# Moving the rotary addition of the local attention from GpSimd to VectorE, and moving three pieces of work to later steps of the stage loop

## The reference

```
def _L0_ffn_ref(x, wqkv, q_scale, k_scale, wo, ln_g, ln_b, w1, b1, w2, b2):
    def l2norm(t):
        return t / jnp.clip(jnp.linalg.norm(t, axis=-1, keepdims=True), 1e-12)
    ...
        q = q * cos * scale + rotate_half(q) * sin * scale
        k = k * cos / scale + rotate_half(k) * sin / scale
    ...
    def _layer(x, ...):
        h = shift_token(x)
        q, k, v = jnp.split(h @ wqkv, 3, axis=-1)
        q = l2norm(q) * qs
        k = l2norm(k) * ksc
        q, k = rotary_xpos(q, k)
        x = x + local_attention(q, k, v) @ wo
        ...
        return x + (a * gelu(g)) @ w2 + b2

x = L0_attn_x
xn = _layernorm(x)
x = x + _L0_attn_ref(xn, ...) * _silu(_L0_ffn_ref(xn, ...))
xn = _layernorm(x)
x = x + _L1_attn_ref(xn, ...) * _silu(_L1_ffn_ref(xn, ...))
```

## Time and profile before

| | |
|---|---|
| three runs | 3027.77, 3028.91, 3041.24 us (median 3028.91) |
| the profiled execution | 3018.12 us, its span 3016.2 us, mean granted TensorE clock 0.959 |
| stage -1 | 0 to 87 us |
| retention stages 0 to 7 | 87 to some 1170 us, 136 us each |
| latent stages 8 to 14 | some 1170 to 2237 us, 157 or 160 us each from stage 9 on |
| stage 15, then the experts | 2237 to 2390 us, then to the end |

### The profile page before, as it was taken

One profiled execution on the slowest core, in us unless ns is written; L12 is line 12 of the kernel. 1 busy time (PEld: TensorE's weight loads), 2 busy tenths in 40 slices (PEclk: granted clock), 3 DMA queues, 4 the chain that ended last, 5 costly groups with the idle time before them and its releaser, 6 DMA issues.

```text
span 3016.2 us, 42014 instructions
## 1 busy us (share of the span) xinstructions
PE 2759.6 (91%) x15582; PEld 1865.9 (62%) x15582; DVE 1613.1 (53%) x3810; ACT 1216.7 (40%) x2249; POOL 1046.1 (35%) x735
## 2 busy tenths in 40 slices
PE   6999999999999999899999999999987899999992
PEld 3575656566565656545555555556554488989992
DVE  6656566675656557666667667675754520000004
ACT  4444444535344445444444445454543242212221
POOL 5423243443423244353534445352532221111113
PEclk9999999999999999999999999999998799999996
DMA  3000000000001011001010101010001367989886
GB/s 135 11 22 18 25 22 32 15 25 15 25 22 47 26 42 65 15 4 50 4 50 4 50 4 43 11 43 12 29 18 36 142 253 269 348 327 350 331 325 209
DMA packets 85908, 261.84 MB, mean 87 GB/s; under 512 B 10668, under 2 KB 49916, under 8 KB 67020
## 3 DMA queue, kind: packets, MB, share of 16 engines
q1 hardware_dynamic: 79228, 241.38, 22.0%
q0 software_dynamic: 6480, 17.77, 1.6%
HBM read 210.81 MB, written 44.11 MB: 85 GB/s over the span
## 4 chain that ended last, share of the span: by engine, by line
PE 74%; DVE 13%; DMA 5%; issue 3%; SPq 2%; POOL 2%; ACT 1%; POOLq 0%; DVEq 0%; ACTq 0%
PE s_pD L705 21%; PE s_pA L705 17%; PE s_pD L1153 7%; PE s_pA L1138 6%; PE s_pD L859 4%; PE s_pD L777 3%; PE s_pA L755 3%; PE s_pA L764 3%; DMA s_w_w<-rows_s 3%; DVE s_pairs L1722 2%; DVE s_qk L1624 2%; PE s_pA L869 2%; PE s_pA L716 2%; PE s_pA L744 1%; DMA s_z<-s_cur 1%
## 5 line engine op out<-in xcount | busy, mean ns | idle before, releaser
L1455 POOL TENSOR_TENSOR s_qk<-s_qk,s_rrec 128x1024 f32<-128x1024 f32 (+1 forms) x128 | 223.5, 1746 | 594.2 <-DVE s_rrec L1630 594.1
L705 PE MATMUL s_pA<-s_w_wqkv,s_curT 128*128 128x512 f32 x768 | 370.5, 625 | 5.6 <-ACT s_curT L1183 3.7
L1207 ACT ACTIVATE s_qk<-s_qk,s_mx 128x256 f32<-128x256 f32 (+1 forms) x512 | 239.8, 471 | 61.6 <-DVE s_mx L1624 60.9
L705 PEld LDWEIGHTS s_pA<-s_w_wqkv,s_curT 128*128 128x128 f32 x768 | 148.5, 199 | 187.4 <-issue 174.6
L1722 DVE TENSOR_SCALAR s_pairs<-s_pD 128x1024 f32<-128x1024 f32 (+1 forms) x192 | 193.6, 1039 | 130.2 <-PE s_pD L859 128.2
L2071 DVE COPY s_w_wo<-s_pD 128x256 f32<-128x256 f32 x71 | 30.0, 423 | 413.8 <-PE s_pD L1124 413.8
L859 PE MATMUL s_pD<-s_mixer 32*128 32x512 f32 (+3 forms) x1024 | 188.8, 486 | 49.8 <-DVE s_pairs L1722 34.3
L1545 POOL DMA_INDIRECT acc_s<-s_w_w,s_sq x71 | 68.5, 964 | 472.0 <-ACT s_w_w L1396 464.7
L1449 POOL TENSOR_TENSOR s_rinv<-s_ssq,s_half 128x16 f32<-128x16 f32 x64 | 204.7, 3198 | 6.4
L859 PEld LDWEIGHTS s_pD<-s_mixer 32*128 32x128 f32 x1024 | 97.1, 196 | 153.4 <-issue 55.1
L1445 POOL TENSOR_TENSOR s_qk<-s_qk,s_rot 128x1024 f32<-128x1024 f32 x64 | 150.7, 2355 | 112.4 <-DVE s_qk L1607 112.4
(11 more groups left out here) (270 smaller groups left out, 5833.3 us busy)
## 6 DMA issues: line engine op xcount, KB each, us to landing
s_qkT<-in_m_w SPq DMA_DIRECT2D x48, 1024.0 KB, 5.1
s_v_tm<-in_m_w SPq DMA_DIRECT2D x24, 1024.0 KB
s_rot<-in_m_w SPq DMA_DIRECT2D x24, 1024.0 KB, 5.6
s_w_wqkv<-in_m_w SPq DMA_DIRECT2D x23, 1024.0 KB
s_qk<-in_m_w SPq DMA_DIRECT2D x23, 1024.0 KB, 5.5
s_w_w<-rows_s SPq DMA_DIRECT2D x71, 129.0 KB
s_cur<-in_x SPq DMA_DIRECT2D x8, 512.0 KB, 3.3
xn_s<-s_cur SPq DMA_DIRECT2D x8, 512.0 KB, 2.6
```

What stands on the lines that cost most here:

```text
L705: last = nc.tensor.matmul(out, lhs(c), rhs(c), start=(c == 0), stop=(c == n - 1))
L1207: last = nc.scalar.activation(pi, pi, ACT.Exp, scale=-1.0, bias=mx[:, u, i:i + 1], accum_out=rsum[:, u, i:i + 1])
L1455: nc.gpsimd.tensor_tensor(pi, pi, rrec[:, u, :].unsqueeze(2).broadcast_to((P, 4, 256 - lo)), ALU.mult).then_inc(p_rdy, 1)
```

## The change

The rotary addition moves to VectorE, and `tiny` goes: its bound becomes an upper bound of 1e12 on the reciprocal norm, inside the scaling. In the stage loop, `down_projection`'s second half moves from u = 1 to 2 in stages 8 to 14 and what hangs on it moves by a step; the transposes of the tokens and the projections behind them move from u = 4 to 5; `input_stats` and `input_apply` move from u = 6 and 8 to u = 8 and 10. The diff, cut (the ring lists and ScalarE's loop follow the same moves):

```
-            def down_projection(b):
+            def down_projection(b, i):
...
-                        down_projection(k)
+                        down_projection(k, 0)
+                        if s.ret or s.last:
+                            down_projection(k, 1)
+                    if s.lat and not s.last and u == 2:
+                        down_projection(k, 1)
...
-                    if s.lat and u == 4:
+                    if s.lat and u == 5:
                         for i in range(2):
                             pe.wait_ge(norm_x, NT * b + 2 * i + 2)
                             pair_transposes("x1T", b, i, lambda t, c: xn[:, t, c * P:(c + 1) * P])
...
                 if w == 1:
-                    act.wait_ge(rinv_rdy, NT * b + 3)
+                    act.wait_ge(rot_rdy, NT * b + NT)
...
-            def rotary_sum(b, t):
-                pool.wait_ge(rot_rdy, NT * b + t + 1)
-                nc.gpsimd.tensor_tensor(qk[:, t, :], qk[:, t, :], rot[:, t % 2, :], ALU.add)
...
-                    if s.ret and k + 2 < B and u == 6:
-                        reciprocal_roots(var_1, rstd_1, k + 2)
-                    if s.lat and u == 2:
-                        reciprocal_roots(var_x, rstd_x, b)
...
                     if s.ahead and u < 2 * NT:
                         scale_probabilities(k + 1, u)
+                    if s.lat and u == 2:
+                        reciprocal_roots(var_x, rstd_x, b)
+                    if s.ret and k + 2 < B and u == 8:
+                        reciprocal_roots(var_1, rstd_1, k + 2)
...
-                if t >= 2:
-                    dve.wait_ge(rinv_rdy, NT * b + t - 1)
...
-                nc.vector.tensor_tensor(o1, o1, Ct[:, t].unsqueeze(2).broadcast_to((P, 2, 8, DH)), ALU.mult).then_inc(rot_rdy, 1)
+                step(nc.vector.tensor_tensor(o1, o1, Ct[:, t].unsqueeze(2).broadcast_to((P, 2, 8, DH)), ALU.mult))
+                nc.vector.tensor_tensor(qk[:, t, :], qk[:, t, :], rot[:, t % 2, :], ALU.add).then_inc(rot_rdy, 1)
                 dve.wait_ge(outA, doneA["qk", b, t])
-                step(nc.vector.tensor_reduce(ssq[:, t, :], heads(sq[:, t % 2, :], 16), AX.X, ALU.add))
-                nc.vector.tensor_tensor(ssq[:, t, :], ssq[:, t, :], tiny[:].broadcast_to((P, 16)), ALU.max).then_inc(ssq_rdy, 1)
+                nc.vector.tensor_reduce(ssq[:, t, :], heads(sq[:, t % 2, :], 16), AX.X, ALU.add).then_inc(ssq_rdy, 1)
...
-                nc.vector.tensor_tensor(heads(qk[:, t, :], 16), heads(qk[:, t, :], 16), per_head(rinv[:, t, :], DH), ALU.mult).then_inc(qk_rdy, 1)
+                dve.wait_ge(rot_rdy, NT * b + t + 1)
+                nc.vector.scalar_tensor_tensor(out=heads(qk[:, t, :], 16), in0=per_head(rinv[:, t, :], DH), scalar=1e12, in1=heads(qk[:, t, :], 16),
+                                               op0=ALU.min, op1=ALU.mult).then_inc(qk_rdy, 1)
...
-                    if s.ret and k + 2 < B and u == 6:
+                    if s.ret and k + 2 < B and u == 8:
                         input_stats(k + 2)
-                    if s.ret and k + 2 < B and u == 8:
-                        input_apply(k + 2)
                     if s.ret and u == 10:
                         ret_out(k, 0)
+                    if s.ret and k + 2 < B and u == 10:
+                        input_apply(k + 2)
...
                         ffn_out(k, 0)
                         gated_sum(b, 0)
+                    if s.lat and u == (1 if s.last else 2):
                         ffn_out(k, 1)
-                    if s.lat and u == 2:
+                    if s.lat and u == (2 if s.last else 3):
                         gated_sum(b, 1)
                         ln_variances(var_x)
-                    if s.lat and u == 3:
+                    if s.last and u == 3:
                         tokens_apply(b)
...
+                    if s.lat and not s.last and u == 4:
+                        tokens_apply(b)
```

More of the change, by code:

```diff
@@ L200, in ring_d_jobs @@
                 j += [("aTM", b - 1, 3)]
-            if s.here and u == 1:
+            if (s.ret or s.last) and u == 1:
                 j += [("w2", k, 0), ("w2", k, 1)]
+            if s.lat and not s.last and u in (1, 2):
+                j += [("w2", k, u - 1)]
             if s.ret and u in (2, 4, 6, 8):
@@ L318, in stream_layers @@
         half = sb("half", [P, 16])
-        tiny = sb("tiny", [P, 1])
         cur = [sb(f"cur{i}", [P, NT, D]) for i in range(2)]
@@ L798, in up_projection @@
                 project(ps[0:n, 0:T], lambda k: W["w1"][:, k, c * HCH:c * HCH + n], lambda k: zT[:, k, :], DC).then_inc(mmD, 1)
-            def down_projection(b):
+            def down_projection(b, i):
                 rows = [min(HCH, HSZ[c] + (c == NHC - 1)) for c in range(NHC)]
-                pe.wait_ge(outD, doneD["a", b, NHC - 1])
-                for i in range(2):
-                    ps = slotD("w2", b, i)
-                    for k in range(2):
-                        last = project(ps[:, k * D:(k + 1) * D], lambda c: hT_of(b)[c][0:rows[c], tile_cols(2 * i + k)], lambda c: W["w2"][0:rows[c], c, :], NHC)
-                    last.then_inc(mmD, 1)
+                if i == 0:
+                    pe.wait_ge(outD, doneD["a", b, NHC - 1])
+                ps = slotD("w2", b, i)
+                for k in range(2):
+                    last = project(ps[:, k * D:(k + 1) * D], lambda c: hT_of(b)[c][0:rows[c], tile_cols(2 * i + k)], lambda c: W["w2"][0:rows[c], c, :], NHC)
+                last.then_inc(mmD, 1)
             def router_product(b):
@@ L1359, in _ @@
                         ret_turned("roT", k, u // 2 - 3)
-                    if s.lat and u == (4 if s.last else 5):
+                    if s.lat and u == 5:
                         router_exp(b)
@@ L1428, in _ @@
             step(nc.gpsimd.memset(half[:], -0.5))
-            step(nc.gpsimd.memset(tiny[:], 1e-24))
             nc.gpsimd.memset(curT[:, :, 0:1], 0.0).then_inc(const_p, 1)
@@ L1495, in _ @@
                     if s.ahead:
-                        rotary_sum(k + 1, t)
-                    if s.ahead:
                         head_norms(k + 1, t)
@@ L2021, in _ @@
                         latent_out(b - 1, u - 3)
-                    if s.last and u == 4:
+                    if s.lat and not s.last and u == 4:
+                        tokens_apply(b)
+                    if s.last and u == 5:
                         router_logits(b)
-                    if s.lat and u == 4:
+                    if s.lat and u == 5:
                         latent_in(b)
                         shared_key(b)
-                    if s.lat and u == 4 and not s.last:
+                    if s.lat and u == 5 and not s.last:
                         router_logits(b)
```

## The result

| | before | after | ratio (95%) |
|---|---|---|---|
| 4 runs each | 3029.9 us median (3027.77 to 3041.24) | 2989.47 us median (2987.63 to 2993.58) | 0.9861 (0.9834 to 0.9888) |
| profiled execution | 3018.12 us | 2987.63 us | |

Between the two profiles it is 30.5 us.

The account below looks back on a forecast made before the run. TensorE, busy 91% of the span, was taken to bound the kernel. Rotary 0, statistics -9, latent stages +6.3 and stage 15 -1.7 summed to -4.4 us: 3024.5 us from 3028.9, range 3006 to 3043 for 8 in 10.

Parts of the forecast that it names:

- -9: Statistics' move in retention stages 0 to 5: 1.5 us gained in each of six stages.
- +6.3: Latent stages 8 to 14: moved steps lose 0.9 us in each of seven stages.
- If a stretch at half rate follows this wait: Retention stages, new wait before the local attention's last product: half rate there takes 1.4 us back, leaving 0.9 gained.
- the two ends: Retention stage's gain: 2.3 us without half rate behind the new wait, 0.9 with it; 1.5 taken.
- The end without half rate, -2.3: Retention stage: the last local attention product begins 2.3 us earlier, with no half rate behind its new wait.
- Rival 1: Faster: no half rate in retention stages (-14), latent chain even or slightly better (-3), some -18 in all; 3010 us, chance 0.23.
- Sum of the waits 6.7 us against 5.86: Latent stage, steps 2 to 5: TensorE's waits grow from 5.86 to 6.7 us, 0.9 lost a stage.
- Four of my waits: Latent stage, TensorE: 1.2 and 0.3 us before half tiles 1 and 2, 1.1 before 3, 2.0 before tokens' transposes.
- So TensorE's 2.27 us stay: Rotary part, ahead of latent scores: the copy starts when it did before, TensorE's wait stays, gain 0.
- Rival 3: Rotary part: VectorE's addition gets the port first, scores' copy comes 1.1 us earlier, -7 to -20; 3008 us, chance 0.06.
- The term -1.7: Stage 15: the latent output's second half runs in the 2.23 us wait for the tokens' norm, gaining 1.7 us.
- draw that costs 0 or some 3 us: Clock: each new TensorE wait may or may not be followed by half rate, costing 0 or some 3 us.

Follow-up runs that it names:

- m3: Kernel before with only the statistics and normalisation moved to steps 8 and 10 in retention stages 0 to 5; 3011.28 us, ratio 0.9958.
- m1: Kernel before with all moves but without the rotary edit; 3002.35 us, ratio 0.9921.
- a1: The full change run again, against the kernel before on the same chip; 2992.07 us, ratio 0.9883.
- x5: Changed kernel with the statistics one step later, at step 9 behind the copy of half tile 6; 2985.1 us, ratio 0.9862 to the kernel before.
- x7: Changed kernel with the down projection undivided at its old step, only the tokens' latent moves left; 2990.9 us, ratio 0.9882 to the kernel before.
- m4: Kernel before with only the moves in the latent stages and stage 15; 3020.31 us, ratio 0.9988.
- c5: Changed kernel with statistics at step 9, second tanh behind half tile 2's exponentials, addition back on GpSimd, small maximum still removed; 2983.62 us.
- c1: Changed kernel with statistics at step 9 and second tanh behind the exponentials of half tile 2; 2961.3 us, ratio 0.9796 to the kernel before.
- c3: As c1, but without the rotary edit (addition on GpSimd, small maximum on VectorE); 2987.86 us, ratio 0.9877 to the kernel before.
- x1: As m3, with the statistics taken a second time at their old place; 3037.42 us, ratio 1.0036 to the kernel before.
- c7: The kernel of c1 run again; 2959.29 us, ratio 0.9779 to the kernel before.

## Why the prediction was wrong

Measured one on top of the other, the statistics' move gives 13 us (m3), the latent moves with stage 15 another 11 (m1) and the rotary edit another 11 (a1), 35 in all. I had -9, +6.3 - 1.7 and 0. In another order the shares differ, since alone the last two give 4 us each.

**Statistics: mechanism right, size wrong.** I took -9 us for six stages; the profiles show 13 (16 against the second profile of the kernel before) and m3 measured 13 (8 to 17). The wait of 2.5 us went and one of 1.50 came where I had put 1.5 to 2.2. The step that failed is "If a stretch at half rate follows this wait [...] 1.4 us go again and 0.9 stay. I take 1.5 us gained, the middle". None follows in the change, and x5 prices the wait at its own length. The middle of the two ends was a value that no stage takes. The end without half rate, -2.3, was near the 2.6 measured. Rival 1 had this part right (-14); no rival reached 2989 us.

**Latent stages: the sign was wrong.** The failed step is "Sum of the waits 6.7 us against 5.86: 0.9 us lost a stage": from stage 9 on it should have been 1.7 us of idle time gained. Four of my waits were too long: 1.2 and 0.3 ahead of the transposes of half tiles 1 and 2, measured 0.90 and none; 1.1 ahead of half tile 3, measured 0.77; 2.0 ahead of the tokens' transposes, measured 0.96, the largest miss. Each link was a little long, and the misses added up: counted from the end of the down projection (1535.8), the tanh began at +0.8 (I had +1.0), the copy at +1.4 (+1.7), the exponentials at +1.8 (+2.3), the maxima of half tile 4 ended at +11.7 (+12.4), and `tokens_apply` took 2.61 us, not 3.21. And I had missed one wait altogether, that of the latent scores for the keys (14.6 us in all before, 8.5 and 2.2 after), because I walked steps 2 to 5 only. That wait was in the list from which I took the earlier trace rows. The waits of 2.07 us and of 2.34 us ahead of the latent scores came as forecast.

**Stage 8 went the other way,** which I had priced like the six others: it is 4.3 us longer. The same stretch of stage 8, before and after:

```profile
1226.30:1381.10 154.80, 141.72 (x801) 84.18 (x801) 104.55 (x241) 73.23 (x125) 68.23 (x49) 0.96 0.04 13
1209.80:1368.90 159.10, 144.39 (x800) 86.46 (x800) 104.62 (x241) 73.08 (x125) 58.13 (x45) 0.94 0.04 13
```

Its idle time rises from 13.1 to 14.7 us; TensorE waits 1.83 and 2.50 us for GpSimd's scaling, where it was 0.34 and 0.84. In x7, without the split, it is idle for 11.5 us, and the five stages behind it for 11.1 or 11.2, where the change has 10.7 to 11.1. So the split saves a little in the later stages and costs 3.2 us in the first. Stages 8 to 13 together took 946.7 us before (949.9 in its second profile) and 941.7 after (942.0), 5 to 8 us less, and their idle time fell by 6 to 7.

**Less idle time isn't always a shorter stage,** which a sum of waits can't hold. m4 has the same latent moves and nearly the same idle time in stages 8 to 13 as the change (69.9 us; the change 68.9, before 75.7), but takes 951.0 us there, with 881.1 us of busy time against 871.0 before, and gained 3.6 us in all (the stages from one profile each). c5 shows it at its clearest.

**Rotary edit: not zero.** TensorE's wait stayed, as predicted, and retention stages didn't change (136.4 and 136.5). The failed step is "So TensorE's 2.27 us stay [...] Sum: 0": it prices the wait and not the products behind it. The two groups behind it run 0.6 and 1.1 us shorter in c1 than in c3, and the stretch 2.1 us; in other stages of the kernels with the edit it is only 0.5 us. The addition took 1.24 us, not 1.50. Rival 3 (the port goes to VectorE first) didn't come: the copy stands where it stood. Why this edit shortens the half rate behind a wait of the same length isn't shown. Candidates are the 0.1 us by which the wait differs and what stands around it in time.

**Stage 15: the wait went, the time didn't.** The wait of 2.23 us fell to 0.51 as I had it, but one for ScalarE's copy into `s_zT` is new:

```profile
2315.13 1.45 PE L717 MATMUL s_pA<-s_ident,s_mixer 128*128 128x128 f32 x8 [0.51 <-DVE s_mixer L1589]
...
2317.97 1.95 PE L706 MATMUL s_pD<-s_mixer,s_zT 128*128 128x8 f32 x16 [1.39 <-ACT s_zT L1265]
```

From the first transposes of the tokens to the products of L834 (now L835) it takes 18.6 us in both profiles. The term -1.7 is not borne out.

**The rest.** The experts and the tail were some 7 us shorter between the profiles. From the down projection of stage 14 to the end the two profiles of the change differ by as much (834.4 and 840.3 us; the kernel before 843.2 and 842.6), so most of it is spread, and I count none of it to the change.

**The clock's share.** 0.9% of the time (c3 against c1) hangs on an edit that moves idle time by 0.8 us a stage. The Trainium skill (TensorE: Matmul & The Clock Gate, What's actually happening) says that the clock follows recent activity on a beat that runs freely. x1 and the two profiles of the kernel before agree; the two of the change, equal stage by stage, show that the outcome can also come again. The Trainium skill (TensorE: Matmul & The Clock Gate, What's actually happening) also puts the ramp at a kernel's start at under 1% of a typical span; no run here prices the start, and most of the 0.9% comes from stages in the kernel's middle.

The prediction named the "draw that costs 0 or some 3 us" after each wait, and then treated it as noise around a sum of waits. That is one root of the miss, beside the waits above: seven latent stages repeat each other, so whatever a stage draws, the others tend to draw too (157.0 five times in c3, 153.6 five times in c7).

## What to carry to other kernels

Sum waits and half rate apart, per repeated stage: length, busy time of the same matmuls, idle time. Here idle time answered to edits as a chain says and busy time didn't, and a stage that repeats multiplies it, so a range has to hold both cases times the number of stages. Walk the first stage of a kind by itself: its waits weren't those of the others. Look at what stands ahead of a link that everything waits for, as the tanh did: moving it brought some 20 us, more than any part of the change. And test a split move by its halves, since one of them may do nothing.

## What the runs showed of the hardware

The same wait of 2.38 us at the same instruction was followed by TensorE at 1.2 GHz in some stages and at 2.4 GHz in others of one execution (x1). Taking out the small maximum alone (c3 to c5; its bound goes into the scaling) shortened a wait from 2.27 to 1.12 us and its stretch by 3.3 us (70.8 to 67.5), and the stretch behind it became 3.4 us longer (86.2 to 89.6): the stage stayed at 157.0 us. The same latent instructions were busy for 870.8 us in m3 and 888.7 in x1 (stages 8 to 13), with idle times of 75.6 and 76.5 us. Latent stages of different kernels came out at few lengths, 153.6, 157.0 and 160.3 us above all; what decides between them stays open.
